# The first item's score maxima moved into the projection stage, and fewer filler matmuls, in a four-stage transformer kernel

## What is computed

```python
x = x + _layernorm(_L1_attn_ref(_layernorm(x, axis=-1), L1_attn_w_qkv), axis=-1)
# per head:  softmax(causal(q @ k.T) / sqrt(8)) @ v
```

## Time and profile before

| | us |
|---|---|
| three runs | 1760.1, 1764.17, 1772.46 |
| median | 1764.17 |
| the profiled execution, its time | 1764.4 |
| the profiled execution, its span in the trace | 1762.7 |
| p1, first work to the last copy of v | 1207.7 to 1243.6 |
| a1, first work to item 0's first score | 1256.5 to 1290.7 |
| am, first work to item 0's first score | 460.7 to 471.3 |

### The profile page before, as it was taken

The page is one execution under the profiler, slowest core; times in us unless marked ns, Lnnn a source line. Parts: engine busy times, 40 slices in busy tenths (PEclk is TensorE's granted clock), DMA queues, the critical chain, the costliest instruction groups (busy, mean ns, idle before and its releaser), DMA issues. The chain is left out here.

```text
span 1762.7 us, 35958 instructions
## 1 busy us (share of the span) xinstructions
PE 1571.2 (89%) x12242; PEld 681.7 (39%) x12242; DVE 1300.1 (74%) x2445; ACT 1125.5 (64%) x1789; POOL 593.7 (34%) x1081
## 2 busy tenths in 40 slices
PE   5899999598699999999998888897699999999787
PEld 3422222144244444444443744455233333333232
DVE  5799999678777777777770547774599999999064
ACT  6699999445155655565556433425258888888655
POOL 5434434676313223222221011113223332333473
PEclk9799999799699999999999999998899999999898
DMA  8733434257212112121200500002522222333201
GB/s 237 164 70 60 73 70 131 68 139 199 58 32 50 44 44 62 33 71 35 51 26 25 191 1 1 0 0 93 149 46 49 47 47 50 52 53 72 62 14 48
DMA packets 88815, 119.69 MB, mean 68 GB/s; under 512 B 23957, under 2 KB 61973, under 8 KB 88422
## 3 DMA queue, kind: packets, MB, share of 16 engines
q1 hardware_dynamic: 86550, 115.00, 27.5%
q10 hardware_dynamic: 2096, 2.47, 0.5%
HBM read 69.74 MB, written 47.58 MB: 67 GB/s over the span
## 5 line engine op out<-in xcount | busy, mean ns | idle before, releaser
L1213 DVE TENSOR_REDUCE o_sb<-ps 128x1 f32<-128x512 f32 (+3 forms) x828 | 682.9, 870 | 135.8 <-PE ps L1005 128.8
L1108 ACT ACTIVATE q_buf<-ps 128x1024 f32<-128x1024 f32 (+1 forms) x768 | 574.0, 912 | 226.7 <-PE ps L976 225.4
L1108 ACT ACTIVATE pr_buf<-ps 128x1024 f32<-128x1024 f32 (+1 forms) x384 | 293.1, 910 | 63.0 <-PE ps L976 63.0
L1027 PE MATMUL ps<-q_buf,v_buf 128*9 128x512 f32 (+7 forms) x2880 | 307.1, 517 | 5.3 <-DVE q_buf L1274 2.3
L1169 POOL TENSOR_SCALAR_AFFINE_SELECT q_buf<-q_buf 128x256 f32<-128x256 f32 (+1 forms) x360 | 176.2, 506 | 393.3 <-ACT q_buf L1108 298.0
L976 PE MATMUL ps<-q_buf 48*128 48x512 bf16 (+7 forms) x1536 | 276.6, 330 | 31.1 <-ACT q_buf L1108 9.4
L1169 POOL TENSOR_SCALAR_AFFINE_SELECT pr_buf<-pr_buf 128x256 f32<-128x256 f32 (+1 forms) x280 | 133.9, 500 | 301.8 <-ACT pr_buf L1108 232.6
L976 PE MATMUL ps<-q_buf,k_buf 49*128 49x512 f32 (+3 forms) x1152 | 207.6, 487 | 0.0
L976 PEld LDWEIGHTS ps<-q_buf 48*128 48x128 bf16 (+1 forms) x1536 | 83.5, 93 | 275.4 <-ACT q_buf L1108 153.5
L1274 DVE TENSOR_SCALAR q_buf<-q_buf 128x1024 f32<-128x1024 f32 x192 | 161.9, 874 | 12.3 <-ACT q_buf L1108 8.1
L1027 PE MATMUL ps<-pr_buf,v_buf 128*9 128x512 f32 (+7 forms) x1728 | 158.4, 459 | 1.8 <-POOL pr_buf L1169 0.9
(11 more groups left out here) (216 smaller groups left out, 1899.0 us busy)
## 6 DMA issues: line engine op xcount, KB each, us to landing
qm_d<-pr_buf SPq DMA_DIRECT2D x80, 128.0 KB, 2.4
q_buf<-qm_d SPq DMA_DIRECT2D x24, 384.0 KB, 5.8
o_d<-pr_buf SPq DMA_DIRECT2D x16, 512.0 KB, 2.7
q_buf<-o_d SPq DMA_DIRECT2D x8, 1024.0 KB, 5.1
q_d<-q_buf SPq DMA_DIRECT2D x48, 128.0 KB, 2.1
k_d<-q_buf SPq DMA_DIRECT2D x48, 128.0 KB, 2.0
q_buf<-q_d SPq DMA_DIRECT2D x60, 96.0 KB
q_buf<-k_d SPq DMA_DIRECT2D x60, 96.0 KB
```

Of the source, the lines that this page charges most:

```text
L1027: mm = nc.tensor.matmul(ps[VW * j:VW * j + V_ROWS_OUT, o_bank + half % O_BUFS, lo * P:(lo + nq) * P], v, units(i, r, j)[:, 0, off * P:(off ...
L1108: nc.scalar.activation(units(i, g, WIDE * e, WIDE), ps[:, bank:bank + WIDE, :], ACT.Exp, scale=scale).then_inc(s_e, 1)
L1213: nc.vector.tensor_reduce(to, sc, AX_X, ALU.max).then_inc(s_mr, 1)
```

## The change

Five edits. (1) In p1, PE and DVE make and reduce the 18 pairs of item 0 of a1 behind the last chunk, in banks 0 to 3, two pairs in flight, without fillers; DVE gathers and turns the result there. (2) The 13 loads of item 0 go from ACT's queue at the end of p1 to SP's queue, behind the stores of chunk 4; item 1's 13 loads and the 8 transfers of minus one, which stood at the head of a1, stand behind the last store of p1 on SP's queue, and SP waits for them before the phase ends. (3) In p1, the copy of the turned chunk goes from ACT to DVE. (4) In p1, the statistics of the last two chunks go from the start into the loop, behind chunks 1 and 2, and their inverses on POOL behind chunks 2 and 3. (5) In a1 and in am, the fillers of the head go. a1 begins with item 1's 8 pairs.

```diff
--- before.py
+++ after.py
@@ -529,6 +529,16 @@
             queue.dma_start(vs8[:, s, :, :], v8_d[bass.ds(n, 1), :, :, :].rearrange("n p k w -> (n p) k w"))\
                 .then_inc(done, 16)
 
+        ahead_next = nc.alloc_semaphore(name="ahead_next")
+        ahead_one = nc.alloc_semaphore(name="ahead_one")
+
+        def load_minus_one(queue, done):
+
+            for s in range(NB):
+                for pr in range(2):
+                    queue.dma_start(ks8[64 * pr + MD:64 * pr + MD + 3, s, :, :],
+                                    minus_one.rearrange("p (a t) -> p a t", a=2)).then_inc(done, 16)
+
         def project_heads8(name, wq, wk, wv, first):
             area_at[0] = 8192
             norm = ChunkNorm(name + "ln", shifted=True)
@@ -550,6 +560,12 @@
             s_vp = count(name + "_vp")
             s_st = [count(name + f"_st{r}") for r in range(PR)]
             READY = 0 if first else LATE
...
+            GROUPS = 2 * ROWS_P
             with nc.Block() as block:
                 @block.vector
                 def _(dve):
@@ -558,8 +574,19 @@
                             dve.wait_ge(ld_x[c], 16)
                         norm.stats(dve, c - READY, tiles(x_res, c))
 
-                    for c in range(READY, min(READY + 4, CHUNKS)):
-                        stats(c)
+                    def copy_turned(c):
+                        dve.wait_ge(s_T, c + 1)
+                        if c > 1:
+                            dve.wait_ge(s_v, c - 1)
+                        nc.vector.tensor_copy(xnT[:, c % 2, :], ps[:, c % 2, :]).then_inc(s_xT, 1)
+
+                    if first:
+                        for c in range(4):
+                            stats(c)
+                    else:
+                        nc.vector.memset(block_max, -3.0e38).then_inc(s_pi, 1)
+                        copy_turned(0)
+                        copy_turned(1)
                     for c in range(CHUNKS):
                         u = c % 2
                         if c > 1:
@@ -581,18 +608,40 @@
                         i.then_inc(s_vp, 1)
                         if first and c + 4 < CHUNKS:
                             stats(c + 4)
+                        if not first:
+                            if c + 2 < CHUNKS:
+                                copy_turned(c + 2)
+                            if c + READY - 1 in range(READY, CHUNKS):
+                                stats(c + READY - 1)
                         if first and c < 8:
                             nc.vector.memset(area[32:64, 1024 * c:1024 * (c + 1)], 0.0)
                     if first:
                         copy_folded(dve)
+                    else:
+                        dve.wait_ge(s_pi, 1)
+                        for k in range(GROUPS):
+                            g, p = divmod(k, 2)
+                            segs, slot_at, whole = MAX_ROWS[g]
+                            sc = ps[:, 2 * (k % 2):2 * (k % 2) + 2, :]
+                            if not whole:
+                                sc = sc.rearrange("p a (b c) -> p a b c", c=P)
+                            heads = slice(2 * p, 2 * p + 2)
+                            to = block_max[:, heads, slot_at] if whole else block_max[:, heads, slot_at:slot_at + 4]
+                            dve.wait_ge(s_m, k + 1)
+                            nc.vector.tensor_reduce(to, sc, AX_X, ALU.max).then_inc(s_mr, 1)
+                        dve.wait_ge(s_mr, GROUPS)
+                        best_of_blocks(mx_sb[:, 0, :].rearrange("p (j q) -> p j q", j=QUAD)).then_inc(s_pm, 1)
+                        dve.wait_ge(s_pm, 1)
+                        nc.vector.transpose(mx_turned[:, :], mx_sb[:, 0, :])
 
                 @block.gpsimd
                 def _(pool):
                     if first:
                         make_constants(pool)
...
                     for c in range(CHUNKS):
@@ -603,10 +652,12 @@
                                                     ALU.subtract).then_inc(s_p3, 1)
                         if first and c + 4 < CHUNKS:
                             norm.inverse(pool, c + 4)
+                        if not first and c - 2 in range(CHUNKS - READY):
+                            norm.inverse(pool, c - 2)
                     if first:
                         make_masks(pool)
                     else:
-                        nc.gpsimd.memset(minus_one, -1.0)
+                        nc.gpsimd.memset(minus_one, -1.0).then_inc(s_one, 1)
 
                 @block.tensor
                 def _(pe):
@@ -640,6 +691,32 @@
                             turn(c + 2)
                     if first:
                         fold(pe)
+                    else:
+                        pe.wait_ge(ahead_item, 16 * LOADS8 * 2)
+                        for k in range(GROUPS):
+                            g, p = divmod(k, 2)
+                            bank = 2 * (k % 2)
+                            if k == 0:
+                                pe.wait_ge(s_xT, CHUNKS)
+                            elif k == 1:
+                                pe.wait_ge(s_r1, 2 * CHUNKS)
+                            else:
+                                pe.wait_ge(s_mr, k - 1)
+                            for q, k0, nk, o_ in MAX_ROWS[g][0]:
+                                masked = k0 + nk - 1 == q
+                                if masked:
+                                    for pr in range(2):
+                                        rows = slice(64 * pr, 64 * pr + 64)
+                                        nc.tensor.matmul(ps[:, bank + pr, (o_ + nk - 1) * P:(o_ + nk) * P],
+                                                         causal_q[rows, :], causal_k[rows, :],
+                                                         start=True, stop=False, skip_group_check=True)
+                                for pr in range(2):
+                                    deep = slice(64 * pr, 64 * pr + MD)
+                                    mm = nc.tensor.matmul(ps[:, bank + pr, o_ * P:(o_ + nk) * P],
+                                                          qs8[deep, 0, p, q * P:(q + 1) * P],
+                                                          ks8[deep, 0, p, k0 * P:(k0 + nk) * P],
+                                                          start=not masked, stop=True, skip_group_check=True)
+                            mm.then_inc(s_m, 1)
 
                 @block.scalar
                 def _(act):
@@ -664,8 +741,9 @@
                         load_middle_weights(act)
                     apply(0)
                     apply(1)
-                    copy_turned(0)
-                    copy_turned(1)
+                    if first:
+                        copy_turned(0)
+                        copy_turned(1)
                     for c in range(CHUNKS):
                         if c + 2 < CHUNKS:
                             apply(c + 2)
@@ -676,15 +754,16 @@
                             act.wait_ge(s_qk, 2 * c + s + 1)
                             nc.scalar.activation(parts[:, c % PR, s, 0, :], ps[:, 2 + 2 * s + u, :], ACT.Copy)\
                                 .then_inc(s_p1, 1)
-                        if c + 2 < CHUNKS:
+                        if first and c + 2 < CHUNKS:
                             copy_turned(c + 2)
                         for s in range(2):
                             act.wait_ge(s_r1, 2 * c + s + 1)
                             nc.scalar.activation(parts[:, c % PR, s, 1, :], rest[:, u, s, :], ACT.Copy)\
                                 .then_inc(s_p2, 1)
-                    for r in range(HALVES):
-                        act.wait_ge(s_st[r], 16 * 7)
-                    load_item8(act, 0, 0, 0, 0, ahead_item)
+                    if first:
+                        for r in range(HALVES):
+                            act.wait_ge(s_st[r], 16 * 7)
+                        load_item8(act, 0, 0, 0, 0, ahead_item)
 
                 @block.sync
                 def _(sp):
@@ -703,6 +782,16 @@
                                     d[b, 2 - part if s else part, :, :, :, :, u * CH:(u + 1) * CH]
                                     .rearrange("d n a h t -> (d n a h) t"),
                                     parts[:, c % PR, s, part, :]).then_inc(s_st[c % PR], 16)
+                        if not first and c == PR:
+                            for r in range(HALVES):
+                                sp.wait_ge(s_st[r], 16 * 7)
+                            load_item8(sp, 0, 0, 0, 0, ahead_item)
+                    if not first:
+                        load_item8(sp, 0, 1, 1, 1, ahead_next)
+                        sp.wait_ge(s_one, 1)
+                        load_minus_one(sp, ahead_one)
+                        sp.wait_ge(ahead_next, 16 * LOADS8)
+                        sp.wait_ge(ahead_one, 16 * 2 * NB)
                     for r in range(PR):
                         sp.wait_ge(s_st[r], 16 * 7 * (CHUNKS // PR))
                     if first:
@@ -887,16 +976,14 @@
```

(35 more changed lines are left out.)

## The result

The changed kernel takes 1760.4 us, the median of 18 runs (1752.7 to 1764.1). The kernel before, run 18 times beside it, takes 1771.7 (1759.4 to 1790.6). The ratio is 0.9934, with its interval from 0.9917 to 0.9951: 0.66% less, or 11.7 us (8.7 to 14.7) of 1771.7. The forecast was 14.7 us less, and "within 1%". Both hold, the first at the edge of the interval. The time itself, 1760.4, lies above the range of 1743 to 1757, mostly because the base isn't 1764.17 but 7.6 us more.

What follows compares the result with a forecast made beforehand. In a1 DVE and PE are nearly always busy, so item 0's start shifts everything; p1's DMA wait and DVE's pairs needlessly follow each other. 13.4 + 1.3 + 0 = 14.7 us off 1764.17 gives 1749.5 us, range 1743 to 1757.

Steps and rivals of the forecast that it cites:

- The base: Whole kernel: savings on the span were taken off the median of the runs, 1764.17 us.
- The clock in am: am's first scores: pairs save 2.0 us, a clock rising no earlier takes back 0.7 (0 to 2.0), leaving 1.3.
- The clock in a1: Item 0's rows in a1: starting at the lower clock costs 0, bounds 1.5 us less and 4 more.
- the 8 us that the prediction allowed: Sign of being wrong: granted clock staying at 0.50 for over 8 us after item 0's first score.
- The dip of before at 1296 to 1300: a1, item 0's rows: the old clock fall to 0.57, costing 1.3 us, need not come behind a cold start.
- p1's loop: p1's chunks: moving the copy off ACT helps only the first chunk; 1.0 us less, bounds 0 and 3.8.
- The tail: p1's end and a1's head: item 0's maxima move behind chunk 7, so its first score comes 13.4 us sooner.
- The barrier: Between p1 and a1: 2.1 us from DVE's turn to PE's first pair, plus 0.3 for clearing a bank.
- The queue: p1's tail: SP's last transfer lands about 1264.9, 1.3 us ahead of DVE's turn, so 21 more transfers cost nothing.
- The rival by which the queue ends last: p1's tail: SP lands at 1268.2, 2 us worse or more, giving about 1752 us; chance 0.21.
- The rival by which the move does little: p1's tail: item 0's loads land behind the stores, pairs start 9 us later, leaving 1758.5 us; chance 0.06.
- more is saved: p1, a1 and am: ACT's chunk shrinks 0.48, no dip, am keeps 2.0; about 1745 us; chance 0.23.

Runs made afterwards that it cites:

- run 18: Not a label but part of "run 18 times": the kernel before, unchanged, was run 18 times beside the changed one; median 1771.7 us (1759.4 to 1790.6).
- e4: The changed kernel run again with nothing edited, on the same chip as three follow-up kernels; ratio to the kernel before 0.9951 (0.9926 to 0.9976).
- e2: The changed kernel with the six fillers put back in am alone; ratio to the kernel before 0.9957 (0.9933 to 0.9982).
- e10: The changed kernel with fillers among the pairs before am and behind am's six pairs; ratio to the kernel before 0.9947 (0.9922 to 0.9973).
- e11: e7 with the fillers of both e9 and e10 added; ratio to the kernel before 0.9963 (0.9935 to 0.999).
- e12: e7 with only e10's fillers added, before and in am; ratio to the kernel before 0.992 (0.9895 to 0.9945).
- e1: The changed kernel with the fillers between item 1's pairs put back in both heads, am and a1; ratio to the kernel before 0.9962 (0.9931 to 0.9992).
- e3: The kernel before with only the fillers between item 1's pairs taken out in both heads, without the move; ratio to the kernel before 1.0007 (0.9976 to 1.0038).
- e8: The changed kernel with the 8 transfers of minus one issued twice on SP's queue; ratio to the kernel before 0.9929 (0.9905 to 0.9954).
- e6: The changed kernel with item 0's 13 loads issued behind chunk 3's stores instead of chunk 4's; ratio to the kernel before 0.9886 (0.9848 to 0.9925).
- e5: The changed kernel with the copy of the turned chunk back on ACT; ratio to the kernel before 0.9907 (0.9872 to 0.9941).
- e7: e6 with item 1's loads and minus one issued on ACT's queue instead of SP's; ratio to the kernel before 0.9898 (0.9863 to 0.9933).
- e9: The changed kernel with fillers from p1's tail into a1, behind the pairs of items 0 and 1; ratio to the kernel before 0.9936 (0.9908 to 0.9964).

## Why the prediction was right in the difference and wrong in the time

**The base.** The step of the prediction that failed is the last one of its sum, "on the median 1764.17 - 14.7 = 1749.5", which took the saving off a base of 1764.17. Three runs from 1760.1 to 1772.5 stood behind that figure; they are among the 18, whose median is 1771.7. Of the 10.9 us between 1749.5 and 1760.4, 7.6 are this. A range built only from the terms of the sum, with no share for a base known from three scattered runs, was too narrow: off 1771.7 the same forecast is 1757.0 and the same range 1750.6 to 1764.6, which holds the measured 1760.4. The mechanism, the maxima laid under p1's tail, held. The other 3.0 us are three terms, each somewhat too good: 1.0 in am, 0.8 in a1 and 0.7 up to a1's first score, with 0.5 us not placed.

**The clock in am.** 2.0 us less for the pairs was exact (10.59 to 8.57). The term for the clock was mis-sized: taken as 0.7 with bounds of 0 and 2.0, it was 2.4 in the first profile and 4.8 in four others (rows of 29.2 for 24.4), and 1.7 on the mean over both sets, so that am gave 0.3 for 1.3. The prediction let the clock rise no earlier than before; counted from the first pair it rose some 13 us in before (by 474), 17 in after (479.5) and 23 in e4 (483). The fillers didn't raise the clock while they ran, as said. Behind them the rise came some 13 us in (before, e2, e10), 20 (e11, e12) or 27 (e1), so it isn't always sooner than without them.

**The clock in a1.** Taken as 0, within -1.5 to +4; it cost 0.8 (a1 rows 16.1 for 15.3). The lower level lasted 10.7 us into item 0's work, beyond the 8 us that the prediction allowed, and that cost little. The dip of before at 1296 to 1300 did not come, as it had argued: 1.00 over 1293 to 1300. It read one row wrongly: 0.89 over the maxima's stretch is a mean of 0.50 and 1.00, so the clock was up in (0.89 - 0.50) / 0.50 = 78% of it, not 89%. Nothing in the sum hangs on that.

**p1's loop.** Taken as 1.0; 0.7 between the means of the profiles, though single ones of one code lie between 34.3 and 35.6.

**The tail.** From p1's start to a1's first score, 13.5 us less where 13.4 were said, but by terms that cancel. Loads took 5.9 us for 5.3, and landing 3.35 for 2.0 (inside its bounds): 2.0 us late. DVE's pace was right, 20.45 us for 20.5, at the granted clock of 0.50. The barrier took 1.3 us from the end of the turn (1271.58 + 0.21) to PE's first pair (1273.11) where 2.4 were taken, and the pairs 8.1 for 8.7. Over four profiles of the same tail the first score comes at 70.3, 12.7 less than in the one of before. That one is a thin base: e3, whose code is the same up to item 0's turn, has the turn at 72.8 us from p1's start, 2.2 us sooner than before's 74.9.

**The queue.** It was said to land 1.3 us ahead of the end of the turn and thus to cost nothing; it cost nothing and had 2.6 us to spare (e8). The rival by which the queue ends last fell for this kernel, and came true in e6 once the loads were moved again. It had taken 2.27 us for three stores of q as the price of a second queue, but three took 2.43 at 1239.07 in the same trace, before ACT issued a load. The rival by which the move does little fell as well; so did "more is saved", for the copy filled a wait (e5).

**The sum.** 12.7 off up to a1's first score, 0.3 in am, 0.8 back in a1's rows: 12.2 us less. The ratio gives 11.7 (8.7 to 14.7). That they lie so near is in part luck: half of e3's 2.2 us on the base makes it 11.1.

## What to carry to other kernels

Two stretches with different bounds that lie one behind the other, one waiting on DMA and one on DVE, are worth laying over each other: here the way from p1's last copy of v to item 0's turn fell from 39.0 to 25.5 us, and what decides the rest is when the last of the first item's loads lands and when the last issue of the queue ends. Time saved just ahead of a rise of the clock was given back here, as far as 14 profiles can tell, so fillers or gaps there should be tried alone before they are counted. A forecast in absolute time needs a base as good as its terms: give the difference first, and put the scatter of the base into the range.

## What the runs showed beyond that

Single profiles scatter by as much as the effect. From the turn in am to p1's start, where the kernels don't differ, the 14 profiles need 711.8 to 722.7 us. Windows of the same 180 us of work, from 190 to 10 us ahead of p1's start, in the changed kernel, its repetition, e7 and e10:

```profile
1021.73:1201.73 180.00, 161.21 (x649) 89.39 (x649) 116.17 (x366) 63.73 (x167) 29.69 (x55) 0.96 0.00 1
```
```profile
1025.67:1205.67 180.00, 163.58 (x645) 91.59 (x644) 115.70 (x365) 62.20 (x158) 28.45 (x53) 0.93 0.00 1
```
```profile
1018.19:1198.19 180.00, 162.06 (x665) 90.30 (x665) 116.36 (x366) 64.03 (x168) 29.64 (x55) 0.97 0.00 1
```
```profile
1028.76:1208.76 180.00, 163.28 (x633) 94.12 (x633) 115.91 (x365) 58.66 (x143) 26.04 (x49) 0.91 0.00 1
```

The same work runs at a granted clock of 0.91 to 0.97, and fewer instructions fit in 180 us where it is low (633 against 665 matmuls). Over the whole stretch the clock is at its lower level for 16.4 to 41.3 us, and in the 14 profiles that time and the length of the stretch go together (a correlation of 0.99): before has 20.4 us of it in 712.0, e10 41.3 in 722.7, so each us at the lower level costs about 0.5. Among the 18 runs of the changed kernel, time and mean granted clock (0.941 to 0.948) have a correlation of -0.93, with 1.5 us less for 0.001 more. When the clock falls in that stretch differs from run to run; why was not tried. It explains how e9's profiled execution can be no longer than the others with 11 us more in its head: it needed 711.9 us here, near the least. It doesn't explain why e9's median of 12 runs is that of e10 beside it (0.4 us less), while e11, with the same fillers, is 9.2 us slower than e12. That stays open: one profile per kernel doesn't say how often its head looks like this.

A filler on a lowered clock takes 1.22 us where it takes 0.70 on the upper one. Under filled pairs no rise came in am (six profiles) and in a1 of e1; it came near 1262.4 in the old a1, 1264.2 in e9 and 1283.2 in e11. What sets these apart isn't shown. Eight small transfers within SBUF cost 5.57 us of issue, 0.70 each, which made a queue the bound in e6.

Loads one chunk earlier, alone or with the second queue (0.9886 and 0.9898), are the fastest seen. Their intervals overlap that of the changed kernel, which did not run beside them. That loads one chunk earlier and the second queue together beat the same kernel without them is shown by e12 against e10 (5.0 us, 2.2 to 6.8), each with am's fillers, and by the heads (65.9 and 66.2 for 69.5 to 71.5). For the earlier loads alone (67.6) only the head shows it.
